# Sums of squares for the second attention's RMS norm: ordinary fp32 products with one column of ones, in place of split squares and a row of sums that is turned

## The chip, the cores and the metric

The kernel runs on one core of a Trainium2 chip. The metric is the device time of one execution in microseconds; the figure for a version is the median of its runs. Engines: TensorE (PE in the profile, its weight loads PEld), VectorE (DVE), ScalarE (ACT), GpSimd (POOL) and SyncE (SP), which only issues transfers.

## The reference, cut to what matters

Four sequences of 256 tokens and 512 features pass through four residual layers, each behind a layer norm: an attention, a gated low-rank expert layer, a second attention with RMS norm on queries and keys, and a feed-forward layer with 4-bit weights. The change lies in the second attention:

```python
def _rmsnorm(t, w):
    inv = jax.lax.rsqrt(jnp.mean(tf * tf, axis=-1, keepdims=True) + EPS)
    return (tf * inv * w)
q = (x @ Wq.T).reshape(b, s, 32, 128)      # 32 query heads
k = (x @ Wk.T).reshape(b, s, 8, 128)       # 8 key heads, 4 queries each
v = (x @ Wv.T).reshape(b, s, 8, 128)
q, k = _rmsnorm(q, q_norm_w), _rmsnorm(k, k_norm_w)
scores = q k^T / sqrt(128) + slope * (j - i), causal
out = softmax(scores) v, then @ Wo.T
```

The mean is over the 128 features of a head, for every token and every head.

## The kernel before

**Tiles and groups.** The attention walks over 8 groups; a group is one key head, its four query heads and its value head. Each gives one tile for each half of the 1024 tokens: K, Q0 to Q3 and V, 128 features (partitions) by 512 tokens (`HALF`), as products of weights with the transposed activations `xt`. To keep precision, operands are split into a rounded part and a rest (`_hi`, `_lo`, type float32r), and a product is three matmuls (`mm3`, L316 to L318). ScalarE writes the rounded part, VectorE the rest. A few products are ordinary fp32 ones: the scores of the first 128 queries (`qt_f` with `kt_f`, L712) and `k_norm` (L784).

**Slots.** The order of the work is written out by hand as lists of steps. A group has four slots, b = 1, 2, 3 and 0 (`slot_steps`), one for each sequence; in a slot the softmax of one sequence, `pv` and `out` of the sequence before, and three projection tiles of the coming half stand in one list, which every engine walks through, doing its own part of each step. In front stand `lead_steps` and `first_slot_steps`, behind `last_slot_steps` and `tail_steps`; the loop of the other slots runs in `turn_loop`.

**Ring.** Tiles come out in a ring of PSUM banks: two main ones, and a side bank (`SIDE`, the third plane of `turned`) for `v_turn`, `k_rms`, `q_rms`, `q_rms_turn` and `k_norm`. TensorE takes a bank when VectorE has freed its last content (`pe_ring_bank`, `s_ring_free`). The last four turns of `transpose` (L798) use the side bank too and wait for the same.

**Sums of squares.** Behind each K and Q tile ScalarE writes the squares into one buffer `sq` (L839). GpSimd splits them into `sq_hi` and `sq_lo` (L574, L575) in two alternating buffers; the next Square waits for this (`s_sq_split`). TensorE sums over the features by a product whose weights `pick` have a one in a single column, so that the sum of a head comes out as one row of 512 tokens: `k_rms` is two matmuls (L751, L752), and `q_rms` takes a pair of heads in four (L762, L763). VectorE copies or adds rows 0 to 4 of the bank into `sumsq` (L950, L954; it is the memory of `xn`). In slots b = 1 and b = 3 `q_rms_turn` turns these rows into columns, with tokens on the partitions, by four small transposes (L774); VectorE makes `ms` of them (mean plus epsilon, L957), takes the inverse root by three Newton steps (`roots`, L349 to L354), and `k_norm` spreads the keys' root to a tile which VectorE multiplies into `k_raw` (L978). A half's `k_rms` comes in the slot of its K tile, `q_rms` for pair 0 at the end of that slot and for pair 1 at the end of the next.

**Constants.** GpSimd makes `pick` by two memsets and a conversion, before the bias table.

Of the kernel before, what the change touches and what calls it, by code (L numbers as in the profile page):

```python
# [28 lines left out]
P = 128  # L29
# [68 lines left out]
def slot_steps(b, rms):  # L98
# [15 lines left out]
    s += [("q_rms_turn", 1 if b == 1 else 0)] if roots else []  # L114
# [28 lines left out]
def last_slot_steps(b, rms):  # L143
# [26 lines left out]
def lead_steps(rms):  # L170


    if rms:
# [3 lines left out]
        s += [("q_rms_turn", 0), ("tile", K, 1, 0), ("roots", 0), ("tile", Q0, 1, 0), ("k_rms", 1)]  # L177
# [19 lines left out]
RING_STEPS = ("tile", "k_rms", "v_turn", "q_rms", "q_rms_turn", "k_norm", "out")  # L197
# [51 lines left out]
def build(nc, x_in, w_attn, w_dense, lora_a, lora_wr, lora_b, norm_w, codes, absmax, kept, out):  # L249

    with ExitStack() as ctx:
# [57 lines left out]
        s_sq_split = sem("s_sq_split")  # L309
# [17 lines left out]
        act_sq, dve_sq, pool_sq, pe_sq = Tally(), Tally(), Tally(), Tally()  # L327
# [178 lines left out]
        pick = sb("pick", [P, 2 * P], F32R)  # L506
# [62 lines left out]
        RING_TURN = [2 * WT + 2 + 2 * BATCH, 2 * WT + 2 + 2 * BATCH + 2 + 4 + 2 + 2]  # L569
# [10 lines left out]
        def attention(layer, scope):  # L580
# [22 lines left out]
            if rms:  # L603
                sq = sb("sq", [P, HALF], F32, scope)
                sq_hi = sb("sq_hi", [P, 2, HALF], F32R, scope)
                sq_lo = sb("sq_lo", [P, 2, HALF], F32R, scope)
# [3 lines left out]
                sumsq = xn  # L610
# [15 lines left out]
            dve_ms = [0]  # L626
# [39 lines left out]
            def dve_lead(dve, step):  # L666
# [4 lines left out]
                elif step[0] == "lead_turn":  # L671
                    for t in step[1]:
                        at = slice(t * P, (t + 1) * P)
                        dve.wait_ge(s_lead_hi, t + 1)
                        nc.vector.tensor_tensor(xt_lo[:, :, at], lead_bank(t).rearrange("p (c q) -> p c q", c=DC),
                                                as_f32(xt_hi[:, :, at]), ALU.subtract).then_inc(s_lead_lo, 1)

            def pe_steps(pe, steps, g, b):
# [3 lines left out]
                for step in steps:  # L682
# [64 lines left out]
                    elif step[0] == "k_rms":  # L747
                        tile = pe_ring_bank(pe, side=True)
                        pe.wait_ge(s_sq_split, pe_sq.value() + 1)
                        row = pick[:, P - HEADS:2 * P - HEADS]  # L750
                        nc.tensor.matmul(tile, row, sq_lo[:, step[1], :], start=True, stop=False)  # L751
                        pe_ring_done(nc.tensor.matmul(tile, row, sq_hi[:, step[1], :], start=False, stop=True))  # L752
                    elif step[0] == "q_rms":
                        _, half, pair = step
# [9 lines left out]
                        pe_ring_done(ins)  # L764
                    elif step[0] == "q_rms_turn":
                        tile = pe_ring_bank(pe, side=True)
                        half = step[1]
                        if b is not None:
                            pe.wait_ge(s_pt_lo, 3 * n)
                        else:  # L770
                            pe.wait_ge(s_ring_free, pe_ring.value() - 1)
                        hold(nc.tensor)
                        for q in range(HALF // P):
                            ins = nc.tensor.transpose(tile[:, q * ROWS:(q + 1) * ROWS],  # L774
                                                      sumsq[0:ROWS, half, q * P:(q + 1) * P],
                                                      ident[0:ROWS, 0:ROWS])
# [26 lines left out]
            def act_steps(act, steps, g, b):  # L803
                n = None if b is None else S0 + 4 * g + b
                for step in steps:
# [23 lines left out]
                    elif step[0] == "tile":  # L829
# [6 lines left out]
                        if rms:  # L836
                            if not isinstance(act_sq.value(), int) or act_sq.value() > 0:
                                act.wait_ge(s_sq_split, act_sq.value())
                            nc.scalar.activation(sq[:, :], tile, ACT.Square).then_inc(s_sq, 1)  # L839
                            act_sq.up()  # L840
# [13 lines left out]
                    elif step[0] in ("k_rms", "q_rms", "q_rms_turn", "k_norm", "out"):  # L854
# [8 lines left out]
            def dve_steps(dve, steps, g, b):  # L863
                n = None if b is None else S0 + 4 * g + b
                for step in steps:
# [82 lines left out]
                    elif step[0] == "k_rms":  # L948
                        tile = dve_ring_tile(dve, side=True)
                        dve_ring_free(nc.vector.tensor_copy(sumsq[0:ROWS, step[1], :], tile[0:ROWS, :]))  # L950
                    elif step[0] == "q_rms":
                        tile = dve_ring_tile(dve, side=True)
                        rows = sumsq[0:ROWS, step[1], :]
                        dve_ring_free(nc.vector.tensor_tensor(rows, rows, tile[0:ROWS, :], ALU.add))  # L954
                    elif step[0] == "q_rms_turn":
                        tile, half = dve_ring_tile(dve, side=True), step[1]
                        dve_ring_free(nc.vector.tensor_scalar(  # L957
                            ms[:, :, :], tile[:, 0:HALF // P * ROWS].rearrange("p (t h) -> p t h", h=ROWS),
# [926 lines left out]
```

## Time and profile before

| | |
|---|---|
| median of 3 runs | 1809.84 us (1807.38 to 1810.34) |
| profiled execution | 1811.87 us |
| its span, first to last instruction | 1810.2 us |
| TensorE busy | 1736.5 us, 96% |
| VectorE, ScalarE, GpSimd busy | 72%, 48%, 44% |
| granted TensorE clock, mean | 0.986 |

The profile records one execution. The span leaves out the start and the end of the program. TensorE's clock has the levels 1.00 (2.4 GHz) and 0.50 (1.2 GHz); the table gives the mean over the span. The second attention lies at about 800 to 1560 us. Matmuls are pipelined, so that the duration of one is longer than the distance to the next.

### The profile page before, as it was taken

To read this page: it belongs to the slowest core of one execution; us is meant where nothing else is said; L and a number is where in the kernel's file an instruction comes from. 1 tells how busy PE (TensorE), PEld (TensorE's weight loads), DVE (VectorE), ACT (ScalarE), POOL (GpSimd) and SP (SyncE) were. 2 spreads that over 40 slices of the span, in tenths; PEclk is the share of its full clock that TensorE was granted. 3 is DMA by queue.
4 is the path that set the end of the run, shared out by engine and by line. 5 is a ranking of instruction groups with operands and counts; after the bars stand their busy time and mean duration, and the time that the engine had idled before them with its cause. 6 is when DMAs were issued, how large, how long until landed. Compare 5 with 4: busy or idle time off the path is not lost.

```text
span 1810.2 us, 28744 instructions
## 1 busy us (share of the span) xinstructions
PE 1736.5 (96%) x8864; PEld 1443.1 (80%) x8864; DVE 1295.3 (72%) x2317; ACT 877.6 (48%) x2288; POOL 787.8 (44%) x924
## 2 busy tenths in 40 slices
PE   8999999999999987997999999999999996899999
PEld 7888888888888877876788888888888885678887
DVE  5788788788878774434777778777878777656555
ACT  3656665665566453222544444444444444544543
POOL 5334436253543542343545445454546333254442
PEclk9999999999999998999999999999999999999999
DMA  4122212221222310000100000000001002022111
GB/s 145 36 70 75 71 57 93 79 66 64 74 65 70 115 53 11 1 29 5 31 30 29 29 29 29 29 29 29 29 29 31 22 9 73 12 66 62 58 58 47
DMA packets 47711, 87.77 MB, mean 48 GB/s; under 512 B 6576, under 2 KB 6576, under 8 KB 47536
## 3 DMA queue, kind: packets, MB, share of 16 engines
q1 hardware_dynamic: 47664, 87.19, 15.2%
q8 instruction: 24, 0.39, 0.1%
q14 instruction: 23, 0.19, 0.0%
HBM read 77.73 MB, written 9.44 MB: 48 GB/s over the span
## 4 chain that ended last, share of the span: by engine, by line
PE 56%; DVE 5%; ACT 3%; POOL 2%; issue 1%; DMA 0%; POOLq 0%; DVEq 0%; ACTq 0%; SPq 0%
PE ring L316 10%; PE ring L318 10%; PE ring L317 10%; PE scores L316 3%; PE scores L318 3%; PE scores L317 3%; PE turned L316 3%; PE turned L318 3%; PE turned L317 3%; PE scores L712 2%; PE turned L798 2%; PE turned L791 1%; PE turned L762 1%; PE turned L763 1%; PE turned L784 1%
## 5 line engine op out<-in xcount | busy, mean ns | idle before, releaser
L316 PE MATMUL ring<-xt_hi,w_lo 128*128 128x512 f32 x768 | 304.6, 397 | 3.9 <-DVE qt_lo L941 1.5
L317 PE MATMUL ring<-xt_lo,w_hi 128*128 128x512 f32 x768 | 303.8, 396 | 0.0
L318 PE MATMUL ring<-xt_hi,w_hi 128*128 128x512 f32 x768 | 303.8, 396 | 0.0
L316 PE MATMUL ring<-wd_hi,ot_lo 128*128 128x512 f32 x512 | 207.5, 405 | 8.8 <-DVE xt_lo L494 3.6
L813 ACT CAST pt_hi<-turned 128x512 fp32r<-128x512 f32 x192 | 100.7, 592 | 234.1 <-PE turned L791 232.4
L317 PE MATMUL ring<-wd_lo,ot_hi 128*128 128x512 f32 x512 | 202.6, 396 | 0.0
L318 PE MATMUL ring<-wd_hi,ot_hi 128*128 128x512 f32 x512 | 202.6, 396 | 0.0
L574 POOL TENSOR_SCALAR sq_hi<-sq 128x512 fp32r<-128x512 f32 x80 | 55.2, 690 | 284.7 <-ACT sq L839 266.3
L316 PEld LDWEIGHTS ring<-xt_hi,w_lo 128*128 128x128 f32 x768 | 145.2, 189 | 36.6 <-DVE qt_lo L941 2.0
L318 PEld LDWEIGHTS ring<-xt_hi,w_hi 128*128 128x128 f32 x768 | 144.8, 189 | 34.7
L317 PEld LDWEIGHTS ring<-xt_lo,w_hi 128*128 128x128 f32 x768 | 144.9, 189 | 31.4
L911 DVE TENSOR_TENSOR p<-p,rsum 128x512 f32<-128x512 f32 (+1 forms) x128 | 150.9, 1179 | 4.4
L550 ACT ACTIVATE lv_early<-code_early 128x512 f32<-128x512 f32 x224 | 123.2, 642 | 54.5 <-POOL code_early L541 53.5
L941 DVE TENSOR_TENSOR qt_lo<-ring,qt_hi 128x512 fp32r<-128x512 f32 x128 | 88.1, 688 | 75.2 <-ACT qt_hi L849 73.7
L873 DVE TENSOR_TENSOR pt_lo<-turned,pt_hi 128x512 fp32r<-128x512 f32 x192 | 120.6, 682 | 24.4 <-ACT pt_hi L813 24.3
L822 ACT ACTIVATE p<-scores,bias,root 128x128 f32<-128x128 f32 (+1 forms) x256 | 128.1, 520 | 19.3 <-DVE bias L901 19.3
L839 ACT ACTIVATE sq<-ring 128x512 f32<-128x512 f32 x80 | 48.4, 605 | 182.1 <-PE ring L318 174.1
L575 POOL TENSOR_TENSOR w_lo<-w_raw,w_hi 128x512 fp32r<-128x512 f32 x96 | 130.5, 1360 | 8.0
L565 POOL TENSOR_TENSOR deq_early<-lv_early 128x512 f32<-128x512 f32 x28 | 37.6, 1341 | 205.4 <-DVE lv_early L559 176.9
L922 DVE TENSOR_TENSOR x<-x,ring 128x512 f32<-128x512 f32 x128 | 87.0, 682 | 52.8 <-PE ring L318 52.3
L316 PEld LDWEIGHTS ring<-wd_hi,ot_lo 128*128 128x128 f32 x512 | 96.4, 188 | 34.8 <-issue 9.3
L899 DVE TENSOR_REDUCE negmax<-scores 128x4 f32<-128x512 f32 (+1 forms) x128 | 121.9, 953 | 2.1
(247 smaller groups left out, 4410.0 us busy)
## 6 DMA issues: line engine op xcount, KB each, us to landing
w_raw<-w_attn_dram SPq DMA_DIRECT2D x96, 256.0 KB, 3.1
wd_raw<-w_dense_dram SPq DMA_DIRECT2D x64, 256.0 KB, 2.7
code_early<-codes_dram SPq DMA_DIRECT2D x28, 256.0 KB, 2.8
absmax_early<-absmax_dram SPq DMA_DIRECT2D x56, 128.0 KB, 3.0
kept_dram<-deq_early SPq DMA_DIRECT2D x28, 256.0 KB, 2.0
stage<-kept_dram SPq DMA_DIRECT2D x28, 256.0 KB, 2.7
code_late<-codes_dram SPq DMA_DIRECT2D x14, 256.0 KB, 2.6
absmax_late<-absmax_dram SPq DMA_DIRECT2D x28, 128.0 KB, 2.9
```

The lines of the kernel that those rows point to most:

```text
L316: nc.tensor.matmul(o, l_lo, r_hi, start=start, stop=False)
L317: nc.tensor.matmul(o, l_hi, r_lo, start=False, stop=False)
L318: return nc.tensor.matmul(o, l_hi, r_hi, start=False, stop=stop)
L550: ins = nc.scalar.activation(lv[:, q, :], code[:, par, :], ACT.Copy, bias=offset, scale=scale)
L575: nc.gpsimd.tensor_tensor(dst_lo, src, as_f32(dst_hi), ALU.subtract).then_inc(sem_done, 1)
L813: nc.scalar.copy(pt_hi[:, j, :, :], turned[:, j, :, :]).then_inc(s_pt_hi, 1)
L822: ins = nc.scalar.activation(pr[:, h, :], sc[:, h, :], ACT.Exp, bias=bias[:, k, h:h + 1], scale=scale, accum_out=sums[:, k, h:h + 1])
L873: nc.vector.tensor_tensor(pt_lo[:, j, :, :], turned[:, j, :, :], as_f32(pt_hi[:, j, :, :]), ALU.subtract).then_inc(s_pt_lo, 1)
L899: dve_link(nc.vector.tensor_reduce(negmax[:, k, :], sc[:, :, :], AX.X, ALU.max, negate=True))
L911: nc.vector.tensor_tensor(pr[:, :, :], pr[:, :, :], rsum[:, k, :].unsqueeze(2).to_broadcast([P, HEADS, width]), ALU.mult).then_inc(s_prob, 1)
L922: dve_ring_free(nc.vector.tensor_tensor(x[:, t, :], x[:, t, :], tile, ALU.add))
L941: dve_ring_free(nc.vector.tensor_tensor(lo, tile, as_f32(hi), ALU.subtract))
```

## The change

The squares of a tile stay as they are, one buffer for each of K and Q0 to Q3. A block of 128 features by 128 tokens of them is the stationary operand of an ordinary fp32 product whose moving operand is a column of 128 ones; the sums come out with the tokens on the partitions, one column of the side bank for each head and block. `k_rms` has four such products and `q_rms` eight. VectorE makes `ms` from the bank at once. `q_rms_turn`, `pick`, `sumsq`, `sq_hi`, `sq_lo`, the splits on GpSimd and the semaphore `s_sq_split` go.

```diff
 slot_steps:
-    s += [("q_rms_turn", 1 if b == 1 else 0)] if roots else []
 last_slot_steps:
-        s += [("q_rms_turn", 1), ("pv",), ("mask", 0)]
+        s += [("pv",), ("mask", 0)]
 lead_steps:
-        s += [("q_rms_turn", 0), ("tile", K, 1, 0), ("roots", 0), ("tile", Q0, 1, 0), ("k_rms", 1)]
+        s += [("tile", K, 1, 0), ("roots", 0), ("tile", Q0, 1, 0), ("k_rms", 1)]
 buffers:
-        pick = sb("pick", [P, 2 * P], F32R)
+        ones = sb("ones", [P, 1])
-                sq = sb("sq", [P, HALF], F32, scope)
-                sq_hi = sb("sq_hi", [P, 2, HALF], F32R, scope)
-                sq_lo = sb("sq_lo", [P, 2, HALF], F32R, scope)
+                sq = sb("sq", [P, V, HALF], F32, scope)
-                sumsq = xn
 TensorE:
+            def pe_sums(tile, row, X):
+                for q in range(HALF // P):
+                    at = q * ROWS + row
+                    ins = nc.tensor.matmul(tile[:, at:at + 1], sq[:, X, q * P:(q + 1) * P], ones[:, :], start=True,
+                                           stop=True)
+                return ins
 k_rms:
-                        pe.wait_ge(s_sq_split, pe_sq.value() + 1)
-                        row = pick[:, P - HEADS:2 * P - HEADS]
-                        nc.tensor.matmul(tile, row, sq_lo[:, step[1], :], start=True, stop=False)
-                        pe_ring_done(nc.tensor.matmul(tile, row, sq_hi[:, step[1], :], start=False, stop=True))
+                        pe.wait_ge(s_sq, pe_sq.value() + 1)
+                        pe_ring_done(pe_sums(tile, HEADS, K))
 q_rms:
-                        pe.wait_ge(s_sq_split, pe_sq.value())
-                        for j in range(2):
-                            h = 2 * pair + j
-                            part = (half + 1 + h) % 2
-                            row = pick[:, P - h:2 * P - h]
-                            nc.tensor.matmul(tile, row, sq_lo[:, part, :], start=j == 0, stop=False)
-                            ins = nc.tensor.matmul(tile, row, sq_hi[:, part, :], start=False, stop=j == 1)
+                        pe.wait_ge(s_sq, pe_sq.value())
+                        for h in (2 * pair, 2 * pair + 1):
+                            ins = pe_sums(tile, h, Q0 + h)
 ScalarE:
-                            if not isinstance(act_sq.value(), int) or act_sq.value() > 0:
-                                act.wait_ge(s_sq_split, act_sq.value())
-                            nc.scalar.activation(sq[:, :], tile, ACT.Square).then_inc(s_sq, 1)
+                            nc.scalar.activation(sq[:, X, :], tile, ACT.Square).then_inc(s_sq, 1)
 VectorE:
-                    elif step[0] == "k_rms":
-                        dve_ring_free(nc.vector.tensor_copy(sumsq[0:ROWS, step[1], :], tile[0:ROWS, :]))
-                    elif step[0] == "q_rms":
-                        rows = sumsq[0:ROWS, step[1], :]
-                        dve_ring_free(nc.vector.tensor_tensor(rows, rows, tile[0:ROWS, :], ALU.add))
+                    elif step[0] in ("k_rms", "q_rms"):
+                        rows = slice(HEADS, ROWS) if step[0] == "k_rms" else slice(2 * step[2], 2 * step[2] + 2)
+                        tile = dve_ring_tile(dve, side=True)[:, 0:HALF // P * ROWS]
                         dve_ring_free(nc.vector.tensor_scalar(
-                            ms[:, :, :], tile[:, 0:HALF // P * ROWS].rearrange("p (t h) -> p t h", h=ROWS),
-                            1.0 / HD, RMS_EPS, ALU.mult, ALU.add))
+                            ms[:, :, rows], tile.rearrange("p (t h) -> p t h", h=ROWS)[:, :, rows], 1.0 / HD, RMS_EPS,
+                            ALU.mult, ALU.add))
 roots:
-                        dve.wait_ge(s_ring_free, dve_ring.turns + dve_ms[0])
+                        dve.wait_ge(s_ring_free, dve_ring.value())
 GpSimd, behind each K and Q tile:
-                            pool.wait_ge(s_sq, pool_sq.value())
-                            if squares_used[0]:
-                                pool.wait_ge(s_ring_full, pool_ring.turns + squares_used[0])
-                            split_steps(pool, sq_hi[:, part, :], sq_lo[:, part, :], sq[:, :], s_sq_split)
```

## Rows read from the trace of the kernel before

**Rows 1.** The page: span, and its part 1 (busy us, share, instructions).
```profile
span 1810.2 us, 28744 instructions
...
PE 1736.5 (96%) x8864; PEld 1443.1 (80%) x8864; DVE 1295.3 (72%) x2317; ACT 877.6 (48%) x2288; POOL 787.8 (44%) x924
```

**Rows 2.** Windows, steady part: us, busy us (count) of each engine, clock, DMA, GB/s.
```profile
873.00:1490.00 617.00, 614.46 (x3179) 507.83 (x3178) 480.10 (x979) 275.95 (x784) 295.88 (x307) 1.00 0.08 26
```

**Rows 3.** Groups by form, TensorE, 870:1490: count, busy us, mean ns, idle.
```profile
L762 PE MATMUL turned<-sq_lo,pick 128*128 128x512 f32 x56 | 22.2, 396 | 0.0
...
L751 PE MATMUL turned<-sq_lo,pick 128*128 128x512 f32 x14 | 6.9, 492 | 2.5 <-DVE ms L957 2.5
L774 PE MATMUL turned<-ident,xn 5*128 5x5 f32 x56 | 5.7, 204 | 0.0
```

**Rows 4.** Timeline of TensorE, end of a slot: start us, us, line, what, count.
```profile
1000.94 0.39 PE L762 MATMUL turned<-sq_lo,pick 128*128 128x512 f32 x1
...
1001.87 0.60 PE L791 MATMUL turned<-ident,p 128*128 128x128 f32 x4
1002.30 1.15 PE L798 MATMUL turned<-ident,p 128*128 128x128 f32 x8
1003.29 1.06 PE L712 MATMUL scores<-kt_f,qt_f 128*128 128x128 f32 x8
```

**Rows 5.** Timeline of TensorE around k_rms, in slot b=1 and in slot b=3.
```profile
1013.59 0.39 PE L318 MATMUL turned<-pt_hi,v_hi 128*128 128x512 f32 x1
...
1014.41 0.39 PE L316 MATMUL ring<-xt_hi,w_lo 128*128 128x512 f32 x1
...
1057.62 0.39 PE L318 MATMUL turned<-pt_hi,v_hi 128*128 128x512 f32 x1
...
1059.05 0.39 PE L316 MATMUL ring<-xt_hi,w_lo 128*128 128x512 f32 x1
```

**Rows 6.** Timeline of TensorE around q_rms_turn, slot b=1.
```profile
1010.98 0.40 PE L318 MATMUL ring<-xt_hi,w_hi 128*128 128x512 f32 x1
...
1011.98 0.40 PE L317 MATMUL turned<-pt_lo,v_hi 128*128 128x512 f32 x1
```

**Rows 7.** Groups by form, 800 to 1510 us: VectorE's read of the q_rms bank.
```profile
L954 DVE TENSOR_TENSOR xn<-xn,turned 5x512 f32<-5x512 f32 x32 | 21.6, 675 | 10.4 <-PE turned L763 10.4
```

**Rows 8.** Timeline of TensorE around k_norm, slot b=1.
```profile
1020.02 1.05 PE L784 MATMUL turned<-ident,root 128*128 128x128 f32 x8
...
1021.15 0.40 PE L317 MATMUL ring<-wd_lo,ot_hi 128*128 128x512 f32 x1
```

**Rows 9.** Timeline of TensorE's weight loads: at q_rms_turn, and at k_rms.
```profile
1011.31 0.32 PEld L774 LDWEIGHTS turned<-ident,xn 5*128 5x128 f32 x4 [0.36 <-issue]
...
1013.84 0.19 PEld L751 LDWEIGHTS turned<-sq_lo,pick 128*128 128x128 f32 x1 [0.29 <-issue]
1013.95 0.19 PEld L752 LDWEIGHTS turned<-sq_hi,pick 128*128 128x128 f32 x1
```

**Rows 10.** Timeline of TensorE, lead-in: its waits, idle us and releaser in brackets.
```profile
822.75 0.77 PE L762 MATMUL turned<-sq_lo,pick 128*128 128x512 f32 x1 [2.55 <-POOL sq_lo L575]
...
847.25 1.16 PE L784 MATMUL turned<-ident,root 128*128 128x128 f32 x8 [1.39 <-DVE xn L950]
...
863.98 0.76 PE L762 MATMUL turned<-sq_lo,pick 128*128 128x512 f32 x1 [2.88 <-POOL sq_lo L575]
```

**Rows 11.** Windows of the lead-in (clock behind POOL), and the timeline in the first.
```profile
823.00:826.00 3.00, 3.00 (x8) 2.32 (x9) 0.68 (x1) 0.00 (x0) 0.00 (x0) 0.50 0.02 5
...
846.00:850.00 4.00, 1.97 (x12) 1.65 (x13) 2.58 (x4) 1.25 (x3) 2.60 (x4) 1.00 0.01 2
...
870.00:873.00 3.00, 3.00 (x26) 2.92 (x25) 2.01 (x4) 1.20 (x3) 2.92 (x4) 0.94 0.40 145
...
823.74 0.63 PE L762 MATMUL turned<-sq_lo,pick 128*128 128x512 f32 x1
824.17 0.63 PE L763 MATMUL turned<-sq_hi,pick 128*128 128x512 f32 x1
```

More of the change, by code:

```diff
@@ L194, in tail_steps @@
     return s
-RING_STEPS = ("tile", "k_rms", "v_turn", "q_rms", "q_rms_turn", "k_norm", "out")
+RING_STEPS = ("tile", "k_rms", "v_turn", "q_rms", "k_norm", "out")
 LEAD_STEPS = ("lead_write", "lead_turn", "warm")
@@ L326, in build @@
         act_hi, dve_hi, dve_chain, pool_chain = Tally(), Tally(), Tally(), Tally()
-        act_sq, dve_sq, pool_sq, pe_sq = Tally(), Tally(), Tally(), Tally()
+        dve_sq, pe_sq = Tally(), Tally()
         pool_w, sp_w = Tally(), Tally()
@@ L748, in pe_steps @@
                         tile = pe_ring_bank(pe, side=True)
-                        pe.wait_ge(s_sq_split, pe_sq.value() + 1)
-                        row = pick[:, P - HEADS:2 * P - HEADS]
-                        nc.tensor.matmul(tile, row, sq_lo[:, step[1], :], start=True, stop=False)
-                        pe_ring_done(nc.tensor.matmul(tile, row, sq_hi[:, step[1], :], start=False, stop=True))
+                        pe.wait_ge(s_sq, pe_sq.value() + 1)
+                        pe_ring_done(pe_sums(tile, HEADS, K))
                     elif step[0] == "q_rms":
-                        _, half, pair = step
+                        pair = step[2]
                         tile = pe_ring_bank(pe, side=True)
                         pe_sq.up(3 if pair == 0 else 2)
-                        pe.wait_ge(s_sq_split, pe_sq.value())
-                        for j in range(2):
-                            h = 2 * pair + j
-                            part = (half + 1 + h) % 2
-                            row = pick[:, P - h:2 * P - h]
-                            nc.tensor.matmul(tile, row, sq_lo[:, part, :], start=j == 0, stop=False)
-                            ins = nc.tensor.matmul(tile, row, sq_hi[:, part, :], start=False, stop=j == 1)
[L764 to L776, printed above, removed]
+                        pe.wait_ge(s_sq, pe_sq.value())
+                        for h in (2 * pair, 2 * pair + 1):
+                            ins = pe_sums(tile, h, Q0 + h)
                         pe_ring_done(ins)
@@ L853, in act_steps @@
                                                    tile.rearrange("p (t d) -> p t d", d=HD)))
-                    elif step[0] in ("k_rms", "q_rms", "q_rms_turn", "k_norm", "out"):
+                    elif step[0] in ("k_rms", "q_rms", "k_norm", "out"):
                         act_ring.take(side=step[0] != "out")
@@ L980, in dve_steps @@
                         dve_top(dve, 4 * g + b - 1, step[1], lv)
-            squares_used, lead2 = [0], [False]
+            lead2 = [False]
             def held(b, X):
@@ L992, in pool_steps @@
             def pool_steps(pool, steps, g, b, refill=True, final=False):
-                if b is not None:
-                    squares_used[0] = pool_ring.n
                 if b is None and rms:
@@ L1005, in pool_steps @@
                         pool_norm(pool, step)
-                    if step[0] in ("k_rms", "q_rms"):
-                        squares_used[0] = pool_ring.n
                     if step[0] == "tile":
                         _, X, half, ahead = step
-                        if rms and X != V:
-                            pool_sq.up()
-                            part = half if X == K else (half + 1 + X - Q0) % 2
-                            pool.wait_ge(s_sq, pool_sq.value())
-                            if squares_used[0]:
-                                pool.wait_ge(s_ring_full, pool_ring.turns + squares_used[0])
-                            split_steps(pool, sq_hi[:, part, :], sq_lo[:, part, :], sq[:, :], s_sq_split)
                         if half == 1 and refill and not held(b, X):
@@ L1796, in _ @@
             pool_a(pool)
-            pool_link(nc.gpsimd.memset(rel[:, 0:2 * P], 0.0))
-            pool_link(nc.gpsimd.memset(rel[:, P:P + 1], 1.0))
-            nc.gpsimd.tensor_scalar(pick[:, :], rel[:, 0:2 * P], 1.0, 0.0, ALU.mult, ALU.add).then_inc(s_const, 1)
+            nc.gpsimd.memset(ones[:, :], 1.0).then_inc(s_const, 1)
             for i, slope in enumerate(alibi_slopes()):
```

17 lines of the change are left out of this document (4 added, 13 removed).

## Prediction

> **What bounds the kernel now.** I read the page first. TensorE is busy for 1736.5 of 1810.2 us and every other engine for far less [rows 1], so time is made or lost on TensorE's queue. The change touches the second attention alone, so I read that stage by windows next: in the steady part, 873 to 1490 us, TensorE is busy 614.5 of 617 us at a granted clock of 1.00, while VectorE is busy 78% and GpSimd 48% of it [rows 2]. The reader is to see that nothing is waited for there: what is added to TensorE's queue in that stretch is added to the time, and what leaves GpSimd or VectorE is worth nothing unless TensorE waited for it. The groups by form then give what the edited steps cost, and how many lie in the steady part: 56 L762 products (two for each `q_rms`, so 28 of these), 14 `k_rms` and 56 L774 turns (four for each `q_rms_turn`, so 14) [rows 3]. Their own durations (396, 492, 204 ns) are no cost: products overlap. The cost of a product in a stream is the distance from start to start, which only the timeline shows.
>
> **What is removed from TensorE.**
>
> `q_rms` before: four products 128x512 run from 1000.94 to the turn's first product at 1001.87, 0.93 us, or 0.233 each [rows 4]. 28 of them: 26.0 us.
>
> `k_rms` before: two products. In the slot b=1 the product before starts at 1013.59 and holds its 0.23, the tile behind starts at 1014.41: 0.59 us. In the slot b=3 the same distance is 1057.62 to 1059.05, less 0.23: 1.20 us [rows 5], because there `k_rms` takes the side bank just after `q_rms_turn` and VectorE has not yet read it (the 2.5 us behind "DVE ms" in the group's row [rows 3]). With no turn the bank's last user is the `q_rms` of the slot before, long read. Seven of each: 7 x (0.59 + 1.20) = 12.5 us.
>
> `q_rms_turn` before: last product of the tile at 1010.98 plus 0.23, then four small turns, then the attention's first product; the second of that starts at 1011.98 [rows 6]. 1011.98 - 0.23 - 1011.21 = 0.54 us, the stop in front and the restart behind included. 14 in the steady part and one in the last group, where it stands ahead of `pv` on the chain as well: 15 x 0.54 = 8.1 us.
>
> The last four turns in `transpose` go to the side bank and wait until VectorE has read it. The eight L798 turns last 1002.30 to 1003.29, 0.99 us, where the four L791 need 0.43 [rows 4], so 0.13 more than their share; about half of that is the longer load of the product behind them, and I count 0.06 as the wait. VectorE's read was 5x512 and 675 ns [rows 7]; it becomes a read of 8 values on each partition, in place of 512, so this 0.06 goes: 28 x 0.06 = 1.7 us.
>
> **What is added to TensorE.** Every sum over 128 tokens is now one full-precision product: it loads a 128x128 block of squares as weights and streams one column of ones. `k_rms` has 4, `q_rms` has 8. How many loads is such a product? The other full-precision products show two: `k_norm` has four and L784 shows eight records, each with its load [rows 8]. So a `q_rms` is 16 loads and a `k_rms` 8; the steady part gets 28 x 16 + 14 x 8 = 560.
>
> What does a load with next to nothing behind it cost? No row of before has a one-column product, so I bound it. Below: the turns L774 stream 5 columns, and four of their loads last 0.32 us in all, with 136 ns for one: (0.32 - 0.136) / 3 = 0.061 us from start to start [rows 9]. Above: the eight records of L784, which stream 128 columns, go from 1020.02 to 1021.15 less 0.23: 0.90 / 8 = 0.112 us [rows 8]. They are nearly two to one, so one has to be chosen. The choice is made by two loads that stand without a short product between them: the loads of L751 and L752 start 0.11 us apart (1013.84, 1013.95), while their 512-column products go on for longer [rows 9]. That is an ordinary load (its record lasts 0.19 us) and it keeps the load path for 0.11 us whatever is streamed; the 0.061 belongs to a turn, whose load record lasts 0.136, 0.05 less. The squares are loaded in the ordinary way. I take 0.111.
>
> The Trainium skill (TensorE: Matmul & The Clock Gate, section "Back-to-back issue gap") lists a product of 1 to 64 columns at about 60 cycles, the 25 ns issue floor, with some 62 ns where the sequencer's microcode issues it. The trace's 5-column turns agree with the 62. By that figure 560 loads would be 34.7 us in place of 62.2 and the change would gain; it counts products without the load in front of each. That result is the first rival below, worked out there from the turns' row.
>
> `q_rms` after: 16 x 0.111 = 1.78, less 0.05 because the turn behind it has the short load: 1.73 us; 28 x 1.73 = 48.4. `k_rms` after: 8 x 0.111 = 0.89; 14 x 0.89 = 12.4. The first load of a block is hidden under the 512-column product ahead of it, and the first load behind the block is not, so the count of loads stays.
>
> **What lies beside.** GpSimd loses the splits of 80 tiles and ScalarE its wait for them. In the steady part TensorE waits for neither, so this is costed at nothing; GpSimd's refills of weights come earlier and wait for TensorE as before. VectorE trades 5x512 reads for small ones and one small `ms` step: nothing, under TensorE. The wait of `roots` is now on VectorE's own last read, and costs at most one small operation there; behind it queue the Newton steps, for which `k_norm` has two `out` tiles of slack. The Square of a tile now goes to a buffer of its own, so no wait appears. TensorE's new waits name ScalarE's Square, which ended long before in every slot but the first.
>
> **The lead-in** (4 `q_rms`, 2 `k_rms`, 1 turn) has real waits: 2.55 us and 2.88 us for `sq_lo`, and between them 1.39 us in front of `k_norm` [rows 10]. If all went, 6.8 us would be won; if none does, the four `q_rms` cost 4 x 0.8 = 3.2 us more, and at the clock's lower level twice that. Behind both waits for `sq_lo` stands another: by the order of the steps the first block also needs the side bank that the turn of V held, and the last is followed by a turn that waits for VectorE, which normalises first. I take 0, with -3 to +4 as bounds.
>
> **Sum.** Added 48.4 + 12.4 = 60.8; removed 26.0 + 12.5 + 8.1 + 1.7 = 48.3; lead-in 0: +12.5 us. The profiled execution took 1811.87 us (span 1810.2 and 1.7 around it), 2.0 us above the median of the three runs, 1809.84. So 1824.4 in the profile's terms and **1822.3 us** as a median, 0.7% slower. Own range of this case: the load at 0.108 to 0.114 is 560 x 0.003 = 1.7 us, the lead-in -3 to +4: 1817 to 1829.
>
> **Rivals.**
>
> *Short loads (the other side).* If a one-column full-precision product keeps the path no longer than the 5-column turns, 0.061, then 560 x (0.111 - 0.061) = 28 us less: 12.5 - 28 = -15.5, 1794 us. It decides below 0.111 - 12.5 / 560 = 0.089 us for one load. For it: the only row with so few columns. Against: the L751 and L752 loads and the length of the load records. Chance 0.09.
>
> *The clock falls.* For 1.7 us of each slot the array now streams almost nothing, directly ahead of 1.4 us of turns. Before, the clock stood at 1.00 through 617 us with no such hole; in the lead-in it went to 0.50 behind the waits of 2.55 and 2.88 us [rows 10, 11]. At the lower level four products cost 0.43 each instead of 0.23 [rows 11], so each microsecond there loses about 0.46; the lead-in's first low stretch lasts over the whole of 823 to 826 us, some 1.5 us lost. If half of the 28 blocks bring that: 14 x 1.5 = 21 us, 1843 us; if all, 1864. Against: from 846 to 850 us TensorE was busy only 1.97 of 4 us and the clock stayed at 1.00 [rows 11], and loads with 5 columns did no harm. Chance 0.12.
> The Trainium skill (same page, "Part 4: PE-mode transpose") says that turns don't count as busy for the clock; by it the hole would be some 3.1 us with every `q_rms` and the clock would fall nearly each time, 28 x 1.5 = 42 us above the sum. Here the clock is back at 0.94 of full from 870 to 873 us [rows 11], behind and in turns for the most part, which speaks against it.
>
> *Four loads for each product,* if one column is not taken in two: 62 us more, 1884 us. L784 speaks against. Chance 0.03.
>
> *Nearly no change.* The lead-in gives its 6.8 us and the reads that VectorE no longer makes give a few tenths in each slot: 12.5 - 7 - 4, 1811 us. TensorE's busy share leaves no such room in the steady part. Chance 0.06.
>
> **How the numbers follow.** The forecast has 0.70. From 1810 to 1845 lie it, most of the last rival and about half of the clock's, some 0.81. A measurement of this kernel tells about 0.2% (3.6 us) from no change. Faster: the short loads and a little of the last, 0.10. Same (1806.2 to 1813.5): 0.05. Slower: 0.85.
>
> **What would show it.** In the timeline behind the last `out` product of a slot: 16 records from start to start 0.111 us and 1.7 to 1.8 us until L791; 8 records in `k_rms`, no idle ahead of it in slot b=3; no L774 and 0.54 us less ahead of `pv`; the clock at 1.00 from 873 us to the tail; slot b=1 longer by about 0.5 us, slots b=2 and b=0 by 0.7 to 0.8, and slot b=3 about as long as before. The prediction is wrong if these loads start less than 0.09 us apart, if more than 16 stand in a block, or if the clock row shows 0.50 in the steady part.

## The result, and the profile after

The changed kernel takes 1822.64 us (median of 4 runs, 1821.41 to 1824.59) against 1809.64 us before; the ratio is 1.0075, with a 95% interval from 1.0058 to 1.0092. It is slower by 0.75%, 13.0 us by the medians; the interval leaves 10 to 17 us open. The forecast was 1822.3.

The page, span and part 1, of the kernel after:

```profile
span 1821.1 us, 29052 instructions
...
PE 1756.2 (96%) x9280; PEld 1491.0 (82%) x9280; DVE 1249.4 (69%) x2301; ACT 877.7 (48%) x2288; POOL 626.7 (34%) x762
```

Against [rows 1] GpSimd is busy 161 us less and VectorE 46 us less, and in the steady part none of it came back as time; TensorE is busy 20 us more. Three lines of `mm3` are L314 to L316 now, the sums are L676, the turns of `transpose` L774 and L781, `k_norm` L767, and the scores L714.

Windows of the kernel after, with columns as in [rows 2]; the steady part last:

```profile
817.00:824.00 7.00, 6.92 (x24) 6.22 (x25) 0.19 (x2) 0.00 (x0) 0.00 (x0) 0.51 0.00 0
...
830.80:837.60 6.80, 6.80 (x24) 5.96 (x24) 0.86 (x2) 0.55 (x1) 0.00 (x0) 0.50 0.00 0
...
847.80:854.60 6.80, 6.80 (x25) 6.03 (x26) 0.17 (x1) 0.00 (x0) 2.25 (x3) 0.50 0.01 2
868.30:875.10 6.80, 5.57 (x26) 5.43 (x27) 3.94 (x6) 2.34 (x4) 4.11 (x6) 0.50 0.26 77
873.00:1490.00 617.00, 617.00 (x3489) 534.81 (x3488) 434.77 (x955) 271.68 (x772) 155.19 (x166) 1.00 0.09 27
```

In the steady part TensorE waits for nothing at all and its clock stands at 1.00, as in [rows 2]. The lead-in is another matter: four stretches of 6.8 us each lie at the lower level; the last of them ends at 875.1, 2 us inside the last row.

The timeline of TensorE at the end of a slot, which answers to [rows 4], and around `k_rms` in slot b=1, which answers to [rows 5]:

```profile
1005.35 0.40 PE L316 MATMUL ring<-wd_hi,ot_hi 128*128 128x512 f32 x1
1005.58 1.84 PE L676 MATMUL turned<-ones,sq 128*128 128x1 f32 x16
1007.29 0.63 PE L774 MATMUL turned<-ident,p 128*128 128x128 f32 x4
1007.76 1.04 PE L781 MATMUL turned<-ident,p 128*128 128x128 f32 x8
1008.63 0.61 PE L714 MATMUL scores<-kt_f,qt_f 128*128 128x128 f32 x4
...
1018.38 0.39 PE L316 MATMUL turned<-pt_hi,v_hi 128*128 128x512 f32 x1
1018.61 0.95 PE L676 MATMUL turned<-ones,sq 128*128 128x1 f32 x8
1019.42 0.48 PE L314 MATMUL ring<-xt_hi,w_lo 128*128 128x512 f32 x1
1019.73 0.40 PE L315 MATMUL ring<-xt_lo,w_hi 128*128 128x512 f32 x1
```

A `q_rms` is sixteen records, two for each sum as forecast. From 1005.58 to the turn it takes 1.71 us, where 1.73 was forecast; read from start to start in the trace, nearly all records are 0.111 or 0.112 us apart. A `k_rms` is eight: from 1018.61 to 1019.73 less the 0.23 of one product, 0.89 us. The turns 1007.29 to 1008.63 take 1.34 us where they took 1.42 in [rows 4]. These 0.08 us fit the 0.06 that the forecast put down to the wait for VectorE's read; nothing else tests that term.

To see where the 10.9 us between the two spans lie I cut both traces at four marks: the second layer's first product, the first tile of the second attention, the second block of turns in it, and the twenty-eighth (26 `q_rms`, 13 `k_rms` and 13 turns later). The table is worked out from start times and clock records of the traces, one trace for each kernel; the last rows are experiments that are told below. The last column is TensorE's time at the lower level between the second and the third mark.

```
lengths in us      first      expert    lead-in and   steady,     rest    low clock in
                   attention  layer     first slot    26 slots            the lead-in
before             677.0      127.5     87.5          574.9       343.2   13.7
after              675.3      126.6     93.8          583.4       342.0   27.3
after_place        677.5      127.5     94.0          586.4       343.1   27.3
before_pad         674.7      125.4     86.6          572.2       341.7   10.2
lead_moved         676.4      126.6     84.1          583.4       343.4   13.7
```

The total fits the forecast, its parts do not: the lead-in cost 6.3 us where 0 was forecast, the steady part 8.5 where the sum's terms give 12.1 for these 26 slots, and 4 us were won in stretches that the change does not touch. The experiments are about these. Each was timed beside the kernel before, whose median was 1812.83 us, 1810.09 us or 1810.86 us on those occasions and not 1809.64; so experiments are compared by their ratios to it, and the changed kernel's is 1.0075.

### The profile page after: what moved, and what is told of

Its sections match the earlier page's. It is cut to its first block, busy times and chain, and to the rows that moved or that the text cites. A ratio compares the mean times of both kernels' runs of the same rounds, so it can differ in the third digit from the quotient of the medians.

```text
span 1821.1 us, 29052 instructions
## 1 busy us (share of the span) xinstructions
PE 1756.2 (96%) x9280; PEld 1491.0 (82%) x9280; DVE 1249.4 (69%) x2301; ACT 877.7 (48%) x2288; POOL 626.7 (34%) x762
## 4 chain that ended last, share of the span: by engine, by line
PE 60%; DVE 5%; ACT 2%; POOL 1%; issue 1%; ACTq 0%; DVEq 0%; POOLq 0%
PE ring L314 11%; PE ring L316 10%; PE ring L315 10%; PE turned L676 4%; PE scores L314 3%; PE scores L316 3%; PE scores L315 3%; PE turned L314 3%; PE turned L316 3%; PE turned L315 3%; PE scores L714 2%; PE turned L781 2%; PE turned L774 1%; PE turned L767 1%; ACT p L805 1%; DVE pt_lo L853 1%
## 5 line engine op out<-in xcount | busy, mean ns | idle before, releaser
L314 PE MATMUL ring<-xt_hi,w_lo 128*128 128x512 f32 x768 | 307.7, 401 | 2.4 <-issue 1.4
L316 PE MATMUL ring<-xt_hi,w_hi 128*128 128x512 f32 x768 | 304.5, 396 | 0.0
L314 PE MATMUL ring<-wd_hi,ot_lo 128*128 128x512 f32 x512 | 205.4, 401 | 9.5 <-DVE xt_lo L492 3.6
L316 PE MATMUL ring<-wd_hi,ot_hi 128*128 128x512 f32 x512 | 202.4, 395 | 0.0
L572 POOL TENSOR_SCALAR w_hi<-w_raw 128x512 fp32r<-128x512 f32 x96 | 64.1, 668 | 338.4 <-PE ring L316 250.1
L316 PEld LDWEIGHTS ring<-xt_hi,w_hi 128*128 128x128 f32 x768 | 145.8, 190 | 34.3
L314 PEld LDWEIGHTS ring<-xt_hi,w_lo 128*128 128x128 f32 x768 | 146.3, 191 | 33.6 <-issue 1.9
L891 DVE TENSOR_TENSOR p<-p,rsum 128x512 f32<-128x512 f32 (+1 forms) x128 | 138.2, 1080 | 4.4
L573 POOL TENSOR_TENSOR w_lo<-w_raw,w_hi 128x512 fp32r<-128x512 f32 x96 | 135.6, 1413 | 8.0
L314 PEld LDWEIGHTS ring<-wd_hi,ot_lo 128*128 128x128 f32 x512 | 96.6, 189 | 34.2 <-issue 10.0
L897 DVE TENSOR_TENSOR ot_lo<-turned,ot_hi 128x512 fp32r<-128x512 f32 x128 | 83.9, 685 | 51.4 <-ACT ot_hi L811 51.0
```

Of the source, the lines that this page charges most:

```text
L314: nc.tensor.matmul(o, l_lo, r_hi, start=start, stop=False)
L316: return nc.tensor.matmul(o, l_hi, r_hi, start=False, stop=stop)
L573: nc.gpsimd.tensor_tensor(dst_lo, src, as_f32(dst_hi), ALU.subtract).then_inc(sem_done, 1)
L891: nc.vector.tensor_tensor(pr[:, :, :], pr[:, :, :], rsum[:, k, :].unsqueeze(2).to_broadcast([P, HEADS, width]), ALU.mult).then_inc(s_prob, 1)
```

## The experiments

### splits_back: GpSimd splits the squares again

```diff
+                        if rms and X != V:
+                            pool_sq.up()
+                            pool.wait_ge(s_sq, pool_sq.value())
+                            split_steps(pool, sq_hi[:, part, :], sq_lo[:, part, :], sq[:, X, :], s_sq_split)
 ... ScalarE, ahead of each Square:
+                                act.wait_ge(s_sq_split, act_sq.value())
```

> The changed kernel, but GpSimd still splits every tile of squares into sq_hi and sq_lo as before (nobody reads them) and ScalarE's next Square waits for that. TensorE's list is untouched. Theory T (GpSimd's splits slowed the 512-column products beside them): the twelve products of an out tile, 2.753 us in the trace after, go back to the 2.81 of before; the half of a group (two slots), 44.87 us after, grows by about 0.28 us, 14 halves 4 us, time about 1826 to 1827. Rival N (TensorE does not feel what GpSimd does): out tiles stay at 2.75, the half at 44.87, time 1822 to 1824, and the 4 us by which the steady part came out cheaper than forecast must come from somewhere else.

Measured: 1825.95 us (6 runs), ratio 1.0074 (1.0057 to 1.0090). GpSimd is at its splits again, and the out tile ahead of `k_norm` takes 2.75 us (1026.89 to 1029.64), what it took after:

```profile
L574 POOL TENSOR_TENSOR sq_lo<-sq,sq_hi 128x512 fp32r<-128x512 f32 x68 | 88.0, 1294 | 5.7
```
```profile
1026.89 0.39 PE L315 MATMUL ring<-wd_hi,ot_lo 128*128 128x512 f32 x1
...
1029.64 0.27 PE L771 MATMUL turned<-ident,root 128*128 128x128 f32 x1
```

The steady part is 583.4 us, as after. Theory T fell: these products do not feel GpSimd's splits. The lead-in became longer in the trace, 97.0 us against 93.8, with 30.7 us at the lower clock against 27.3; the ratios of the two kernels, 1.0074 and 1.0075, do not show it. So the splits were worth nothing in the steady part, and at most some 3 us in the lead-in, where a new wait of 1.20 us stands in the trace.

### wide64: 64 columns of ones

```diff
-        ones = sb("ones", [P, 1])
+        ones = sb("ones", [P, 64])
-                    at = q * ROWS + row
-                    ins = nc.tensor.matmul(tile[:, at:at + 1], sq[:, X, q * P:(q + 1) * P], ones[:, :], start=True,
+                    at = (2 * q + row % 2) * 64
+                    ins = nc.tensor.matmul(tile[:, at:at + 64], sq[:, X, q * P:(q + 1) * P], ones[:, :], start=True,
 ... and VectorE reads one column of each 64
```

> The changed kernel with a moving operand of 64 columns of ones instead of one; the sums come out 64 times side by side and VectorE reads one of each. Theory L (the weight load sets the price): 64 columns stream behind the next load, the records stay 0.111 to 0.112 us apart, q_rms stays 1.70 us, the half of a group 44.87. Rival S (the column count counts too): records further apart, up to 0.13, 560 x 0.02 = 11 us more. For the lead-in theory C (one-column blocks keep the clock at its lower level because the array streams nothing): the low stretches of the lead-in, 27.3 us in four pieces after against 13.6 in three before, shrink, and the time falls by 2 to 6 us, to 1817 to 1821. Rival: they stay, and the time stays at 1822.6.

Measured: 1828.12 us (6 runs), ratio 1.0080 (1.0061 to 1.0098). A block in the timeline of TensorE, and two windows:

```profile
1007.89 1.89 PE L676 MATMUL turned<-ones,sq 128*128 128x64 f32 x16
```
```profile
818.90:825.80 6.90, 6.90 (x24) 6.03 (x24) 0.17 (x1) 0.00 (x0) 0.00 (x0) 0.51 0.00 0
873.00:1490.00 617.00, 617.00 (x3474) 532.35 (x3473) 431.89 (x949) 268.80 (x759) 156.75 (x167) 1.00 0.09 27
```

The block lasts 1.73 us up to the turn instead of 1.70: theory L holds, the load sets the price. Theory C fell in this form: the lead-in kept its four low stretches. The half of a group was 45.11 us and not 44.87, of which 0.05 lie in its two blocks and the rest outside them, the out tiles being back at 2.81 us. Outside the blocks the kernel differs from the changed one in little but where its buffers lie.

### q_twice and q_twice_wide: blocks of 32 loads, with one column and with 64

```diff
-                        for h in (2 * pair, 2 * pair + 1):
+                        for h in (2 * pair, 2 * pair + 1, 2 * pair, 2 * pair + 1):
                             ins = pe_sums(tile, h, Q0 + h)
```

> The changed kernel with each q_rms product made twice into the same place, 32 loads in a block instead of 16. Load at 0.111: 28 x 16 x 0.111 = 50 us more in the steady part, 5 to 14 in the lead-in, 1878 to 1886 in all, if the clock stays at 1.00 in the steady part. Clock rival: a hole of 3.5 us in each slot brings the clock down in the steady part, at about 0.46 us lost for each low microsecond; 28 blocks with 3.4 us or more low each: 40 to 90 us on top, 1920 to 1980, and the window row shows less than 1.00.

> q_twice with 64 columns of ones: 32 loads in a block, each with 64 columns. Theory: what counts for the clock is what streams, so with 64 columns (about half of the load's 0.111 us) the clock stays at 1.00 in the steady part: halves of a group at about 45.1 + 3.5 = 48.6 us throughout, time near 1880. Rival (only the loads or the kind of product count): the clock falls as in q_twice, halves of 50 to 54 us, 1930 or more.

Measured: q_twice 1929.49, 1937.39 and 1943.39 us (a fourth run took 10187 us, for which I have no explanation, and stays out of the ratio), ratio 1.0689 (1.0651 to 1.0727); q_twice_wide 1883.91 us (2 runs), ratio 1.0405 (1.0373 to 1.0437). The same window of q_twice and then of q_twice_wide:

```profile
873.00:1490.00 617.00, 615.68 (x3362) 546.27 (x3361) 373.07 (x811) 237.32 (x662) 140.37 (x150) 0.91 0.08 26
```
```profile
873.00:1490.00 617.00, 615.16 (x3615) 535.98 (x3613) 402.72 (x882) 253.51 (x720) 158.76 (x169) 1.00 0.09 27
```

The blocks of q_twice and what follows them, in the timeline:

```profile
1003.77 3.63 PE L676 MATMUL turned<-ones,sq 128*128 128x1 f32 x32
1007.25 0.64 PE L774 MATMUL turned<-ident,p 128*128 128x128 f32 x4
1007.73 1.60 PE L781 MATMUL turned<-ident,p 128*128 128x128 f32 x8
```

With blocks of 3.5 us of one-column products the clock comes down in the steady part: 0.91 on the mean. It does not behind every block: halves of a group take from 48.45 us, which is the price of the loads alone, to 54.45. The steady stretch of 26 slots takes 684.8 us, where 583.4 and 416 more loads at 0.111 make 629.6; the 55 us left lie beside 116 us of lower clock, 0.48 for each, near the 0.46 that the forecast took from [rows 11]. With 64 columns behind the same loads the clock stays at 1.00 and every half of a group takes 48.65 to 48.69 us. So the clock rival of the forecast is real as a mechanism: in the steady part it did not come about with the blocks of the change, came about with blocks twice as long, and not with 64 columns in these.

### before_no_turn: the old sums without their turns

```diff
-    s += [("q_rms_turn", 1 if b == 1 else 0)] if roots else []
-        s += [("q_rms_turn", 1), ("pv",), ("mask", 0)]
+        s += [("pv",), ("mask", 0)]
-        s += [("q_rms_turn", 0), ("tile", K, 1, 0), ("roots", 0), ...
+        s += [("tile", K, 1, 0), ("roots", 0), ...
-                        dve.wait_ge(s_ring_free, dve_ring.turns + dve_ms[0])
+                        dve.wait_ge(s_ring_free, dve_ring.value())
+                        dve_link(nc.vector.memset(ms[:, :, :], 1.0))
```

> The kernel before without the q_rms_turn steps; the roots step works on constants, so the RMS norm is left out. One part of the change alone. By the terms of the sum: 15 x 0.54 for the turns and 7 x 0.60 for the bank that k_rms waited for, 12.3 us less, 1797 us; k_rms shows no idle ahead of it in slot b=3. Rival: the stop ahead of pv stays without the turn, because pv waits as well, and only the 0.34 us of the turns themselves are won: 15 x 0.34 + 4.2 = 9 us, 1800 us.

Measured: 1802.99 us (4 runs), ratio 0.9954 (0.9936 to 0.9972), 8 us less with an interval of 5 to 12. Its `k_rms` in slot b=3, in the timeline, to be held against the third and fourth of [rows 5]:

```profile
1048.43 0.40 PE L317 MATMUL turned<-pt_hi,v_hi 128*128 128x512 f32 x1
1048.66 0.39 PE L750 MATMUL turned<-sq_lo,pick 128*128 128x512 f32 x1
1048.89 0.39 PE L751 MATMUL turned<-sq_hi,pick 128*128 128x512 f32 x1
1049.13 0.39 PE L315 MATMUL ring<-xt_hi,w_lo 128*128 128x512 f32 x1
```

1048.43 to 1049.13 less 0.23 is 0.47 us, two products and no more, where it was 1.20. The half of a group went from 44.22 us on the mean to 43.44, 0.78; the terms of the sum (0.54 and half of 0.60) make 0.84, the rival's (0.34 and half of 0.60) 0.64. So the removal side of the forecast holds in the steady part, a little too high. The whole kernel won 8 us where 12.3 was expected, and the interval just leaves 12.3 out; by that number alone the rival's 9 us would be as good.

### after_place and before_pad: only the places of the buffers

`pick` has 1024 bytes of each partition and `ones` takes 32, so the change also moves all buffers that are laid out behind it, `ot_hi` and `ot_lo` among them. In the kernel before `ot_hi` starts at byte 187552, an odd multiple of 32; in the one after at 186560, a multiple of 64; in wide64 at 186784, an odd multiple of 32 again.

```diff
 after_place, against the changed kernel (ot_hi at 187552):
-        ones = sb("ones", [P, 1])
+        ones = sb("ones", [P, 2 * P])      # only the first column is used
 before_pad, against the kernel before (ot_hi at 187584):
         pick = sb("pick", [P, 2 * P], F32R)
+        pad = sb("pad", [P, 1])            # never used
```

> The changed kernel with the buffer of ones as large as pick was (1024 bytes of each partition instead of 32), so that all buffers behind it, ot_hi and ot_lo among them, lie where they lay before: at an odd multiple of 32 bytes (ot_hi 187552) and not at a multiple of 64 (ot_hi 186560). Nothing else. Theory P (the place of an operand sets a few ns of each product): the out tiles are 2.81 us again as in before and wide64, the half of a group goes from 44.87 to about 45.1, and the first attention, which has the same out tiles, ends 1 to 2 us later: time 3 to 6 us above the changed kernel, 1826 to 1829. Rival (the 2.752 us come from what VectorE or ScalarE no longer do beside the products): 2.752 and 44.87 stay.

> The kernel before with one unused buffer of 32 bytes behind pick, which moves the buffers behind it by 32 bytes (ot_hi 187584, a multiple of 64). Nothing else. Theory P: out tiles 2.752 us, pv 0.03 longer, a half group from 44.25 to about 44.0, the steady part 3 us shorter, the first attention 1 to 2 us shorter: 4 to 5 us less than before in all, ratio 0.997. Rival: no difference, ratio 1.000.

Measured: after_place 1830.51 us (4 runs), ratio 1.0112 (1.0092 to 1.0131); before_pad 1802.32 us (9 runs), ratio 0.9956 (0.9938 to 0.9975). The start of an out tile and of `k_norm` behind it, in the timelines of TensorE of after_place and then of before_pad:

```profile
1026.07 0.40 PE L314 MATMUL ring<-wd_hi,ot_lo 128*128 128x512 f32 x1
...
1028.89 0.27 PE L767 MATMUL turned<-ident,root 128*128 128x128 f32 x1
```
```profile
1011.15 0.40 PE L316 MATMUL ring<-wd_hi,ot_lo 128*128 128x512 f32 x1
...
1013.91 0.28 PE L785 MATMUL turned<-ident,root 128*128 128x128 f32 x1
```

Twelve products take 2.82 us in the one and 2.76 in the other. Theory P holds both ways: the steady part is 3.0 us shorter from after_place to after and 2.7 from before to before_pad, as expected, and the first attention 2.1 and 2.3 us, where 1 to 2 were expected. The whole gain is 6.7 and 8.0 us by the ratios, above the 3 to 6 and the 4 to 5 that were expected, but the intervals of the ratios reach down to these. By the spans of single traces it is 7.4 and 9.6, and not all of that is the place: in the expert layer after has 7 us more at the lower clock than after_place, and before_pad 3 us less than before. At equal places the change costs 1.0112, 20 us (17 to 24); after against before_pad, the other pair of like places, gives 1.012 by the two ratios. The places gave some 7 us of that back.

At equal places the parts of the forecast can be held against the slots. Counted from one block of turns to the next, the slots b = 1, 2, 3 and 0 took 22.79, 21.16, about 23.4 and 21.16 us before and 23.22, 21.86, 23.24 and 21.89 in after_place: 0.7 more in b=2 and b=0, 0.4 in b=1 and 0.2 less in b=3, where the forecast said 0.7 to 0.8, 0.5 and about nothing.

### lead_moved: the two blocks of the lead-in away from their waits

The waits of TensorE in the lead-in of the kernel after, in the timeline, which answers to [rows 10]:

```profile
817.08 3.57 PE L676 MATMUL turned<-ones,sq 128*128 128x1 f32 x16 [2.39 <-DVE v_lo L925]
...
830.56 3.22 PE L676 MATMUL turned<-ones,sq 128*128 128x1 f32 x16
...
847.70 3.48 PE L676 MATMUL turned<-ones,sq 128*128 128x1 f32 x16 [1.87 <-DVE k_raw L951]
864.24 1.92 PE L676 MATMUL turned<-ones,sq 128*128 128x1 f32 x16 [0.61 <-ACT sq L820]
869.53 0.69 PE L746 MATMUL turned<-ident,vt 128*128 128x128 f32 x2 [3.37 <-DVE ms L931]
```

As forecast, the wait for `sq_lo` went and the ones behind it stayed: the side bank (2.39 us) and VectorE's normalising (3.37). What was not foreseen are the durations: three of the four blocks take 3.2 to 3.6 us. They run at the lower clock, and while they do their records are 0.213 us apart.

```diff
-        s += [("q_rms", 0, 0), ("tile", Q2, 0, 0), ("tile", Q3, 0, 0), ("norm_turn", 3), ("q_rms", 0, 1)]
+        s += [("tile", Q2, 0, 0), ("q_rms", 0, 0), ("tile", Q3, 0, 0), ("norm_turn", 3), ("q_rms", 0, 1)]
-        s = [("q_rms", 1, 0), ("tile", Q2, 1, 0)] + softmax[0] + ...
+        s = [("tile", Q2, 1, 0), ("q_rms", 1, 0)] + softmax[0] + ...
```

> The changed kernel with two blocks of q_rms moved: the first of the lead-in behind the tile Q2 and that of the first slot behind its tile Q2, where squares and side bank are long ready. Theory C2 (the clock falls where a wait and a block of one-column products lie side by side, and rises late because such a block follows at the lower level): the two low stretches around 817 to 824 and 848 to 855 go or shrink, TensorE's low time in the lead-in falls from 27.3 us to about 13, time 4 to 8 us below the changed kernel, 1815 to 1819. Rival (the waits alone bring the clock down): low stretches as before and 0 to 2 us won.

Measured: 1816.39 us (7 runs), ratio 1.0033 (1.0017 to 1.0049). Its timeline and windows:

```profile
818.30 1.84 PE L676 MATMUL turned<-ones,sq 128*128 128x1 f32 x16
...
825.69 1.84 PE L676 MATMUL turned<-ones,sq 128*128 128x1 f32 x16
...
845.67 1.84 PE L676 MATMUL turned<-ones,sq 128*128 128x1 f32 x16
```
```profile
817.00:824.00 7.00, 6.47 (x39) 5.40 (x37) 1.78 (x4) 2.47 (x7) 0.00 (x0) 1.00 0.00 0
841.00:846.00 5.00, 4.77 (x16) 3.83 (x16) 0.17 (x1) 0.14 (x1) 2.27 (x3) 0.66 0.02 3
847.00:855.00 8.00, 8.00 (x48) 7.03 (x48) 5.62 (x14) 1.59 (x8) 3.83 (x4) 1.00 0.14 33
```

The blocks are back at 1.84 us for sixteen records, the low clock of the lead-in at 13.7 us, that of the kernel before, and the lead-in at 84.1 us, 9.7 less than after. 13.6 us of lower clock at 0.46 are 6.3 of them; 2.4 are the first wait, which the moved tile now fills, and 1.0 is left over.

The doubled low time is not a matter of one trace. With blocks of sixteen loads in their old places it was 27.3 us in after, after_place and wide64 and 30.7 in splits_back; with the old sums it was 13.7, 10.2 and 6.8 (before, before_pad, before_no_turn). The mean granted clock of the whole kernel was 0.980 to 0.984 in the four runs of after, and 0.984 to 0.990 in fifteen runs of before. What the block and what the wait does to it is not parted, though. The move took the first wait away together with the block; and where a wait stayed, the 1.86 us that now stand ahead of the tile Q2, the clock fell behind it all the same, only for 3.4 us (the window from 841 to 846) and not for 6.8. The old sums had the wait of 2.55 us in three traces, and the clock fell behind it in one.

How after comes to stand 6.3 us above before in the lead-in is worked out, not measured by itself: TensorE's waits of over 0.15 us there add up to 13.5 us before and 10.0 after, which about pays for the longer blocks (4 x 0.8 us), and 13.6 us more at the lower clock make 6.3.

### one_load and one_load_moved: one pass for each sum

```diff
-                sq = sb("sq", [P, V, HALF], F32, scope)
+                sq = sb("sq", [P, V, HALF], F32R, scope)
-        ones = sb("ones", [P, 1])
+        ones_f = sb("ones_f", [P, 16])
+        ones = sb("ones", [P, 2], F32R)
...
-                    ins = nc.tensor.matmul(tile[:, at:at + 1], sq[:, X, q * P:(q + 1) * P], ones[:, :], start=True,
+                    ins = nc.tensor.matmul(tile[:, at:at + 2], sq[:, X, q * P:(q + 1) * P], ones[:, :], start=True,
```

> The changed kernel with the squares rounded to float32r as ScalarE writes them and two float32r columns of ones: one load and one pass for each sum in place of two, so the rest of each square behind the rounding is left out of the sum. ot_hi stays at a multiple of 64 bytes (186624). By the load price: q_rms 8 x 0.111 = 0.89 us and k_rms 0.44, 280 loads less in the steady part, 31 us less; the lead-in loses its four long blocks at the lower level, 5 to 8 us more. 1784 to 1788 us, ratio to before 0.986 to 0.988, and 14 to 18 us below the kernel before with the same placement (before_pad, 1802.3). Rival (the ordinary fp32 kind of product sets the 0.111, not the load; a float32r product of two columns costs another time): at 0.061 a load the steady part falls 14 us more, near 1772; at 0.2 nothing is won.

> one_load with the two blocks of the lead-in and the first slot moved behind the tile Q2, as in lead_moved. If the lead-in of one_load still has low stretches beside its waits, 2 to 6 us less than one_load, 1779 to 1785 us; if its short blocks no longer keep the clock down, no difference.

Measured: one_load 1786.00 us (5 runs), ratio 0.9867 (0.9843 to 0.9891); one_load_moved 1783.79 us (5 runs), ratio 0.9849 (0.9832 to 0.9867). One block of one_load in the timeline:

```profile
1012.92 0.95 PE L677 MATMUL turned<-ones,sq 128*128 128x2 f32 x8
1013.73 0.44 PE L775 MATMUL turned<-ident,p 128*128 128x128 f32 x2
```

Eight records 0.111 to 0.112 us apart, for another kind of product and two columns: the price again is the load's. The steady stretch is 27.8 us shorter than after, where 260 loads less at 0.111 make 28.9. Both kernels beat the kernel before and the one after, but the place of the buffers has its part in it: `ot_hi` lies at a multiple of 64 here, and against before_pad, which has that too, one_load is 16 us faster and not 24. They differ from the reference's arithmetic in that what is lost when a square is rounded to float32r stays out of its sum. Moving the blocks took the lead-in from 84.4 to 79.8 us in the traces, and its time at the lower clock from 20.5 to 13.7 us; the intervals of the two ratios overlap, so the times alone do not show it.

## Why the forecast came out right, point by point

**The price of a load** was the step on which the sign hung, and it held: 0.111 us chosen, 0.111 to 0.112 measured with one, two and 64 columns, in blocks of 4, 8, 16 and 32. The short turns' 0.061 did not apply; all this at a granted clock of 1.00, for at 0.50 the loads of the lead-in are 0.213 us apart. By the figure of the Trainium skill weighed there (TensorE: Matmul & The Clock Gate, "Back-to-back issue gap"), 25 or 62 ns for so few columns, the change would have gained; the measurement decides against using it where each product brings its own weights. The same page of the Trainium skill, section "LDWEIGHTS (loading the stationary operand)", gives the number of columns over 1.2 in ns, 107 for 128 columns; that is near the 0.111 us at full clock, and does not hold for the 0.213 at the lower level.

**Two loads for a sum** in ordinary fp32: held, sixteen records in a block.

**What is removed**: before_no_turn gives 0.78 us for the half of a group where 0.84 was worked out, and 8 us in all (5 to 12) where 12.3 was expected. The wait of `k_rms` in slot b=3 was the bank's, as said.

**The steady part**: at equal places it grew from 574.9 to 586.4 us, 11.5 us; the terms give 12.1 for the same slots, and slot by slot they fit as well. Mechanism and size right.

**What lies beside**: costed at nothing, and nothing it is in the steady part (splits_back).

**The lead-in** is the step that failed: "I take 0, with -3 to +4 as bounds", and it cost 6.3 us. The waits behind the waits were read rightly. What was left out is that with the blocks of one-column products beside these waits the time at the lower clock doubled, from 13.7 to 27.3 us; the forecast looked for this in the steady part alone, gave it 0.12 there, and it did not happen there, though doubled blocks bring it about (q_twice). Which of block and wait does how much stays open.

**Not in the sum at all** was where the buffers lie: 7 us to the good. The two omissions cancelled. The forecast of 12.5 us was met by 12.8 (against the median of 1809.84), and that it was met so closely is luck: for the algorithm alone, at equal places, it would have been 20.3 against 12.5, right in sign and short by the lead-in, and 1830.51 us (after_place) lies outside the range of 1817 to 1829.

## What to carry to other kernels

A product with few moving columns costs its weight load, here 0.111 us for each load with 1 to 64 columns behind it, and an ordinary fp32 product has two loads. In this kernel, putting the larger operand in as weights paid only with one load for each product (one_load). Look also at blocks of such products that stand right behind a wait: here the time at the lower clock was twice as long with them, and moving two of them behind a tile gave that back. When a change adds or removes a buffer, look at where the others move, or hold their places fixed while comparing: here 32 bytes were worth 0.4% (0.2 to 0.6).

## What the runs showed of the hardware that was not expected

- The place of operands in SBUF changes the rate of TensorE's products: twelve 512-column products of the out tile ahead of `k_norm` take 2.81 to 2.82 us with `ot_hi` at an odd multiple of 32 bytes (before, after_place, wide64, q_twice_wide; 2.79 in before_no_turn) and 2.74 to 2.76 at a multiple of 64 (after, splits_back, before_pad, lead_moved, q_twice, both one_load kernels). In the whole kernel 32 bytes made 1810.09 us into 1802.32, a ratio of 0.9956 (0.9938 to 0.9975). Whether 64 bytes is the step that matters, and which of the buffers that move together does it, was not tried; the moving operand `wd_hi` stays in its place, so for the out tiles the one loaded as weights is the likelier. Why the place matters is not known.
- The clock fell in the steady part with blocks of 3.5 us of loads with one column each (116 us low in 26 slots, 0.91 on the mean from 873 to 1490), and not with 64 columns behind the same loads, nor with blocks of 1.7 us. In the lead-in 64 columns did not help (27.3 us low in wide64 as in after); why is open.
- The Trainium skill (TensorE: Matmul & The Clock Gate, "Part 4: PE-mode transpose") says that turns do not count as busy for the clock in the same way. In the kernel after, each 1.7 us block is followed by 1.3 us of turns, 28 times, at a clock of 1.00, so what the forecast made of that sentence, a fall nearly every time, did not come about. No run here sets turns against idle time.
